# One phase for all ghost FFNs, mLSTM units between the MLP tiles of the block in front, and a look-up spread over six stages

## The chip, the cores and the metric

The kernel runs on one core of a Trainium2 chip. The metric is device time in microseconds of one execution. TensorE is PE in the rows (PEld is its weight load), VectorE is DVE, ScalarE is ACT, GpSimd is POOL, SyncE is SP.

## What is computed

```python
x = L0_attn_x                                # (4, 1024, 512) f32
xn = layernorm(x)
x = x + mlstm_block(xn) + ghost_ffn(xn)

def mlstm_block(x):                          # 8 heads, dqk 32, dv 64
    h_in = rmsnorm(x, norm1_w)
    q, k, v, o_pre = h_in @ wq, h_in @ wk, h_in @ wv, h_in @ w_og
    i_pre, f_pre = softcap(h_in @ w_ig + b_ig), softcap(h_in @ w_fg + b_fg)
    Fcum = cumsum(log_sigmoid(f_pre))
    Dmat = where(causal, Fcum[s] - Fcum[t] + i_pre[t], -inf); m = max_t Dmat
    C = (q @ k.T / sqrt(32)) * exp(Dmat - m)
    h = (C / max(|sum_t C|, exp(-m))) @ v
    x1 = x + (sigmoid(o_pre) * rmsnorm_per_head(h) * mh_w) @ w_out
    h2 = rmsnorm(x1, norm2_w)
    return x1 + (silu(h2 @ w_gate) * (h2 @ w_up)) @ w_down      # 2048 wide

def ghost_ffn(x):                            # 1376 wide; weights are looked up
    g, u = x @ lut[gate_idx].T, x @ lut[up_idx].T               # lut has 16 entries
    return (silu(g) * u) @ lut[down_idx].T
```

## The kernel before, in words

The 4096 rows are taken in eight blocks of 512 rows (`TOK`), two halves for each of four sequences; `at = (b, half)` names one. Everything is fp32 precision on fp32r matmuls: each operand is kept as a rounded part (`hi`) and the remainder (`lo`), and `split` does three matmuls for one product.

Both FFNs are cut into tiles of 128 hidden columns: 11 ghost tiles (`NF`, the last one padded) and 16 MLP tiles (`NM`). A tile is the same for both: `gate` (12 matmuls of 512 columns into `gate_bank`), `up` (12 into `up_bank`), `tanh` on ScalarE, `gated` and `product` on DVE, `hid` on ScalarE (hi part of the hidden) and on POOL (its lo part, line 1757), and `down` (12 into the four accumulators `acc`), which comes one tile later. The weights of a tile, hi and lo, are read from scratch tensors in HBM, 1 MB for gate and up (`load_gu`, line 445) and 0.5 MB for down (`load_dn`, line 450), into two slots each. `load_gu` of tile t+1 waits for `up` of tile t-1.

A stage of a block has three parts. `front`: gate logits, then twelve projections of 128 rows (q and k, v, output gate; line 549 with `attn_w`), and beside them the chain of rows for the exponents (DVE lines 1359 to 1405, ScalarE lines 963 to 1034, transposes on TensorE). The row scratch lies in the x buffer of the other half (`rows`, `og`), so the front waits on DVE until that buffer's output has been stored (lines 1353 to 1356). `ghost`: the 11 ghost tiles of this block; eight mLSTM units (four row blocks, two groups of four heads) run between their matmuls, in an order written out in `units` (line 745): `unit_1` (exponents, scores) after gate, `unit_2` (values) after up, `unit_3` (state) after down, then head transposes, output projection and h2. On DVE the unit's work stands around `gated` and `product` (lines 1558 to 1605). Then come the 16 MLP tiles of the same block on h2, with the layer norm and transposes of the next block's x in the last ones (`mlp_ends`, `x_T`), and at the end DVE adds the accumulators to the residual (`add_out`, line 1641), which ScalarE stores in four transfers (line 1151).

The ghost weights do not exist at the start. They are looked up in 33 chunks of 128x512 (`NCH`: gate, up and down of each tile): ScalarE computes eight levels from bit 0 of the index and pairs of table entries (`level`, line 924), DVE takes the three other bits (line 1281) and chooses with seven `copy_predicated` (line 1302), 10 steps a chunk and one more for bit 0 (line 1293); then ScalarE rounds (`upper`, line 929), POOL subtracts (line 1745) and stores the pair from its own DMA queue (line 1752). `plan` spreads these steps: chunks 0 to 20 in stage 1, 21 to 32 in stage 2, 10 steps in each unit. For that reason stage 1 has no ghost tiles; those of block 0 come last of all (`LAST`, lines 837 to 845 and 1664 to 1671), from its transposed x that is made a second time, and with its rows kept in `first_rows`. The MLP weights are split in stage 1 as well (ScalarE line 937, POOL line 1734, DVE lines 1312 and 1317), the first MLP pass computes from the freshly split tiles, and SP stores them for the later stages. The look-up's work space lies over the projection weights, which are stored once and loaded back (`reload_w`).

SP issues nearly all loads in one queue, in the order of the program: a wait in it holds up every later load. At the end of each second stage SP also waits until the last rows were stored (line 522). All engines run loops over the sequences 1 to 3, so stages 3 to 8 are one code.

## Time and profile before

| | us |
|---|---|
| median of 3 runs | 2777.57 (2776.36 to 2778.02) |
| the profiled execution | 2779.31 |
| its span, first to last instruction | 2777.5 |

| engine | busy us | share of the span |
|---|---|---|
| TensorE, matmuls | 2493.6 | 90% |
| TensorE, weight loads | 2000.8 | 72% |
| DVE | 1295.4 | 47% |
| ScalarE | 809.4 | 29% |
| POOL | 598.7 | 22% |

The shares are means over stages with different limits: a stage has to be read in its own window. In the rows of a timeline the columns are start and length in us, engine, line, operation, output<-input and count; in brackets stands how long the engine was idle before it and which event ended that. Rows with a q behind the engine are what its queue issues, DMAs above all. Line 549 is the helper for all tiled products, so its rows are told apart by the names of the tiles.

### The profile page before, as it was taken

How to read it: one execution, taken by the hardware profiler on the slowest of the kernel's cores; microseconds unless marked ns; L12 is line 12 of the kernel's file. 1: busy time of each engine (PE TensorE's matmuls, PEld its weight loads, DVE VectorE, ACT ScalarE, POOL GpSimd, SP SyncE). 2: the span in 40 equal slices, each digit the busy share in tenths (PEclk: the TensorE clock that was granted, in tenths of full speed). 3: DMA queues.
4: the chain of work that ended last, by engine and by line, in shares of the span. 5: the costliest groups of instructions: out<-in, count | busy, mean ns of one | idle time of the engine just before them, and what ended most of it. 6: DMA issues, size and time to landing. Idle time of an engine off the chain costs nothing.

```text
span 2777.5 us, 32515 instructions
## 1 busy us (share of the span) xinstructions
PE 2493.6 (90%) x11024; PEld 2000.8 (72%) x11024; DVE 1295.4 (47%) x2240; ACT 809.4 (29%) x1474; POOL 598.7 (22%) x497
## 2 busy tenths in 40 slices
PE   4545877677999999999999999999999999999988
PEld 3324656566777788778877788778877888778877
DVE  6886874776134632364125622364235523463221
ACT  4653535552114211321123211321123211321111
POOL 1332540322111211131112211121112211121111
PEclk8757999889999999999999999999999999999999
DMA  5213765335542354244542355135533455135544
GB/s 198 72 46 122 283 235 197 129 122 224 193 173 92 137 189 182 83 141 167 200 153 91 129 197 197 72 134 188 184 128 107 152 189 196 62 138 188 194 182 154
DMA packets 95754, 431.78 MB, mean 155 GB/s; under 512 B 10496, under 2 KB 10496, under 8 KB 65664
## 3 DMA queue, kind: packets, MB, share of 16 engines
q1 hardware_dynamic: 80400, 393.56, 39.3%
q10 hardware_dynamic: 10464, 19.14, 2.1%
q0 software_dynamic: 4752, 17.30, 1.6%
q8 instruction: 78, 1.28, 0.2%
q14 instruction: 60, 0.49, 0.1%
HBM read 371.77 MB, written 58.20 MB: 155 GB/s over the span
## 4 chain that ended last, share of the span: by engine, by line
issue 52%; PE 16%; POOL 9%; ACT 3%; DVE 2%; DMA 2%; POOLq 0%; ACTq 0%; DVEq 0%; SPq 0%
POOL hidden_lo L1757 5%; PE acc L549 4%; PE up_bank L549 3%; PE gate_bank L549 3%; PE bank_b L549 3%; PE bank_a L549 2%; ACT look_w L924 1%; POOL MX L1770 1%; POOL vw L1785 1%; DMA gu<-gu_parts 1%; POOL rh L1702 1%; POOL rs L1702 1%; DMA first_rows<-xn 1%; DVE look_w L1281 0%; PE gate_bank L583 0%
## 5 line engine op out<-in xcount | busy, mean ns | idle before, releaser
L1757 POOL TENSOR_TENSOR hidden_lo<-hm,hidden_hi 128x512 fp32r<-128x512 f32 x216 | 279.6, 1294 | 1504.8 <-ACT hidden_hi L866 1504.7
L549 PE MATMUL acc<-dn,hidden_hi 128*128 128x512 f32 x1728 | 548.0, 399 | 24.6 <-POOL hidden_lo L1757 24.6
L1325 DVE SCALAR_TENSOR_TENSOR th<-th,gate_bank 128x512 f32<-128x512 f32 x216 | 147.8, 684 | 642.6 <-ACT th L861 642.6
L549 PEld LDWEIGHTS acc<-dn,hidden_hi 128*128 128x128 f32 x1728 | 324.0, 191 | 93.1 <-issue 20.2
L866 ACT ACTIVATE hidden_hi<-hm 128x512 fp32r<-128x512 f32 x216 | 135.9, 629 | 848.0 <-PE acc L549 824.2
L549 PE MATMUL gate_bank<-hT_hi,gu 128*128 128x512 f32 x1024 | 340.9, 394 | 30.4 <-DVE hT_lo L1547 19.4
L549 PE MATMUL up_bank<-hT_hi,gu 128*128 128x512 f32 x1024 | 339.7, 393 | 0.7 <-DVE hm L1331 0.6
L549 PE MATMUL acc<-dn,hidden_lo 128*128 128x512 f32 x864 | 339.6, 393 | 0.0
L861 ACT ACTIVATE th<-gate_bank 128x512 f32<-128x512 f32 x216 | 128.8, 596 | 471.8 <-PE gate_bank L549 471.8
L1331 DVE SCALAR_TENSOR_TENSOR hm<-th,up_bank 128x512 f32<-128x512 f32 x216 | 148.0, 685 | 241.6 <-PE up_bank L549 241.0
L549 PE MATMUL up_bank<-xT_hi,gu 128*128 128x512 f32 x704 | 256.8, 426 | 0.0
L549 PE MATMUL gate_bank<-xT_hi,gu 128*128 128x512 f32 x704 | 242.3, 405 | 8.2 <-DMA gu<-gu_parts 8.2
L549 PEld LDWEIGHTS gate_bank<-hT_hi,gu 128*128 128x128 f32 x1024 | 194.0, 189 | 77.1 <-issue 23.5
L549 PEld LDWEIGHTS up_bank<-hT_hi,gu 128*128 128x128 f32 x1024 | 193.1, 189 | 43.3 <-DVE hm L1331 3.3
L924 ACT ACTIVATE look_w<-look_w,lt,ld 128x512 f32<-128x512 int32 x208 | 156.0, 805 | 180.7 <-DMA gu_parts<-look_w 64.7
L549 PE MATMUL gate_bank<-hT_lo,gu 128*128 128x512 f32 x512 | 200.8, 392 | 0.0
L549 PE MATMUL up_bank<-hT_lo,gu 128*128 128x512 f32 x512 | 199.8, 390 | 0.0
L549 PEld LDWEIGHTS acc<-dn,hidden_lo 128*128 128x128 f32 x864 | 164.5, 190 | 35.6
L549 PEld LDWEIGHTS up_bank<-xT_hi,gu 128*128 128x128 f32 x704 | 132.9, 189 | 40.2 <-issue 13.7
L549 PEld LDWEIGHTS gate_bank<-xT_hi,gu 128*128 128x128 f32 x704 | 133.1, 189 | 36.3 <-DMA gu<-gu_parts 8.6
L1302 DVE COPY_PREDICATED look_w<-look_w 128x512 f32<-128x512 int32 x182 | 139.2, 798 | 2.4
L549 PE MATMUL up_bank<-xT_lo,gu 128*128 128x512 f32 x352 | 138.4, 393 | 0.0
(233 smaller groups left out, 3711.3 us busy)
## 6 DMA issues: line engine op xcount, KB each, us to landing
gu<-gu_parts SPq DMA_DIRECT2D x200, 1024.0 KB, 4.8
dn<-dn_parts SPq DMA_DIRECT2D x200, 512.0 KB, 3.4
gu_parts<-gu SPq DMA_DIRECT2D x16, 1024.0 KB, 6.3
gu_parts<-look_w POOLq DMA_DIRECT2D x17, 512.0 KB, 3.1
ix<-idx ACTq DMA_DIRECT2D x33, 256.0 KB, 2.7
raw_gu<-w_gu SPq DMA_DIRECT2D x16, 512.0 KB, 6.9
qkT<-x SPq DMA_DIRECT2D x8, 1024.0 KB, 6.1
xn<-x SPq DMA_DIRECT2D x8, 1024.0 KB, 7.9
```

Source lines behind the costliest of these rows:

```text
L549: mm = pe.matmul(dst, l[a], r[c], start=first and k == 0 and n == 0, stop=last and k == len(lhs) - 1 and n == 2)
L861: act.activation(th[:], GB[:], ACT.Tanh, scale=0.5).then_inc(act_tanh.sem, 1)
L866: act.activation(HH[0][:], hm[:], ACT.Copy).then_inc(act_hid.sem, 1)
L924: act.activation(level_of(n, k), bit0_of(n), ACT.Identity, bias=lt[:, 2 * k:2 * k + 1], scale=ld[:, k:k + 1])\
L1302: dve.copy_predicated(level_of(n, lower), bit_of(n, bit), level_of(n, upper)).then_inc(look_vec, 1)
L1325: dve.scalar_tensor_tensor(th[:], th[:], 1.0, GB[:], ALU.add, ALU.mult).then_inc(vec_gate.sem, 1)
L1331: dve.scalar_tensor_tensor(hm[:], th[:], 0.5, UB[:], ALU.mult, ALU.mult).then_inc(vec_hm.sem, 1)
L1702: pool.tensor_tensor(dst, src, half_pow[:, 0:n], ALU.pow).then_inc(stage.sem, 1)
L1757: pool.tensor_tensor(HH[1][:], hm[:], HH[0][:].bitcast(f32), ALU.subtract).then_inc(pool_hid.sem, 1)
L1770: pool.tensor_tensor(MX[0:n, :, :], mhl[0:n, j * P:(j + 1) * P].unsqueeze(1).to_broadcast([n, H, P]), hm32[0:n, 0:H].unsqueeze(2).to_broad ...
L1785: pool.tensor_tensor(vw[:, u % 2, :, :], va[:, c:c + HG * VS].rearrange("p (h n) -> p h n", h=HG), rn[:, f:f + HG].unsqueeze(2).to_broadca ...
```

## The change

- Two phases. Phase one has a stage per block: `front`, then the 16 MLP tiles of the block **before** it with this block's eight units, output projection and h2 in tiles 0 to 10 (`tiles(at)`, with `mb = previous(at)`). The first stage has units alone, and a `TAIL` of 16 plain MLP tiles ends the phase. Phase two has the 11 ghost tiles of all eight blocks, one after the other; each block's last four tiles carry the transposes of the next block's x.
- x and h2 parts share two pairs of buffers (`XH`), one per half. x1 and the MLP result of a block go to scratch rows in HBM (`x1_rows`, `mlp_rows`); phase two loads x, x1 and MLP rows again, 3 MB a block besides the x of the next, and adds them to the ghost result on DVE in tile 3 and at the end. DVE copies the accumulators out at the end of a stage, and SP stores them in one transfer; the next front waits for it (`st_mlp`).
- The look-up moves from stages 1 and 2 to stages 3 to 8: in each of three pairs of stages one third of the matrices, 5 chunks in even and 6 in odd stages, `TAKEN` DVE steps behind each tile's work: 4 (or 5) in tiles 0 to 7, 4 in tile 8, none in 9 and 10, the rest in 11 to 13. Its space lies over the v and output-gate weights, which are loaded back, 4 MB, at the end of each of these stages. SP stores the chunks in place of POOL, two or more tiles later in its queue.
- The MLP splits stand in stage 1, one in each of tiles 0 to 10, and five in the front of stage 2; all are on ScalarE and POOL now. Stage 2 loads tile 0 back once all are stored.

```diff
-NCH = 3 * NF
-PHASES = [0, 4, 21, 24, NCH]
+NCH = NF
+CHUNKS = [(0, 5), (5, NF)]
+TAKEN = [[4] * 8 + [4, 0, 0, 5, 5, 4, 0, 0], [5] * 8 + [4, 0, 0, 5, 6, 5, 0, 0]]
...
@@ block.sync
+            def tiles(at):
+                b, half = at
+                mb = previous(at)
+                stored = 0
+                for t in range(NM):
+                    if t + 1 < NM:
+                        load_gu(MLP, mb, t + 1)
...
+                    else:
+                        load_gu(MLP, at, 0)
+                    load_dn(MLP, mb, t)
+                    if here(at, TAIL):
+                        continue
+                    if t == 8:
+                        wait(sp, vec_norm, at, NB - 1, "gated")
+                        load_next(at)
+                    if t == 11:
+                        wait(sp, vec_x1, at, NB - 1, "x1")
+                        sp.dma_start(rows_of(x1_rows, (b * HALVES + half) * TOK), XN[half][:]).then_inc(st_x1, 16)
+                    if looks(at):
+                        ready = steps_taken(half, t - 1) // STEPS_V if t else 0
+                        for n in range(CHUNKS[half][0] + stored, ready):
+                            store_chunk(at, n)
+                            stored += 1
+                        if t == NM - 1:
+                            for n in range(*CHUNKS[half]):
+                                if n >= CHUNKS[half][1] - 2:
+                                    pair_stored(sp, at, n)
+                            reload_vo(1)
+                            reload_vo(2)
+                wait(sp, vec_out, mb, NB - 1)
+                first = (b * HALVES + half) * TOK + -TOK
+                sp.dma_start(rows_of(mlp_rows, first), XN[half][:]).then_inc(st_mlp[half], 16)
...
+            sp.wait_ge(st_x1, 16 * BATCH * HALVES)
+            for z in range(2):
+                sp.wait_ge(st_mlp[z], 16 * BATCH)
+                sp.wait_ge(ld_vo[z], 32 + 32 * HALVES * (BATCH - 1))
+            with sp.Fori(BATCH, 2 * BATCH) as b:
+                for half in range(HALVES):
+                    at = (b, half)
+                    for t in range(NF):
+                        if t + 1 < NF:
+                            load_gu(GHO, at, t + 1)
+                        else:
+                            load_gu(GHO, (b, half + 1), 0)
+                        load_dn(GHO, at, t)
+                        if t == 0:
+                            wait(sp, pe_xT, (b, half - 2), NB - 1)
+                            load_next(at)
+                            first = (b * HALVES + half) * TOK + -BATCH * SEQ
+                            sp.wait_ge(st_out[half], b * 16 + (16 - BATCH * 16))
+                            sp.dma_start(rest[half], rows_of(x, first)).then_inc(ld_rest[0], 16)
+                            sp.wait_ge(vec_rest.sem, vec_rest.before(at))
+                            sp.dma_start(rest[2], rows_of(x1_rows, first)).then_inc(ld_rest[1], 16)
+                            sp.dma_start(rest[3], rows_of(mlp_rows, first)).then_inc(ld_rest[2], 16)
+                    wait(sp, vec_out, at, NB - 1)
+                    sp.dma_start(rows_of(out, first), rest[half]).then_inc(st_out[half], 16)
...
@@ block.tensor
+                for t in range(NM):
+                    gate(MLP, mb, t, act, stage)
+                    for f, a in fill.get((t, 0), []):
+                        f(at, a)
+                    up(MLP, mb, t, act, stage)
+                    for f, a in fill.get((t, 1), []):
+                        f(at, a)
+                    if stage and t == NM - 1:
+                        x_T(at, 0, XN[1 - at[1]])
+                        x_T(at, 1, XN[1 - at[1]])
+                    if t:
+                        down(MLP, mb, t - 1, NM - 1)
+                    for f, a in fill.get((t, 2), []):
+                        f(at, a)
...
+            tiles(TAIL)
+            with pe.Fori(BATCH, 2 * BATCH) as b:
+                for half in range(HALVES):
+                    at = (b, half)
+                    act = XH[half]
+                    for t in range(NF):
+                        gate(GHO, at, t, act)
+                        up(GHO, at, t, act)
+                        if t >= NF - NB:
+                            x_T(at, t - NF + NB, XN[1 - half], ghosts=True)
+                        if t:
+                            down(GHO, at, t - 1, NF - 1)
+                    down(GHO, at, NF - 1, NF - 1)
...
@@ block.scalar, at the end of a tile, ahead of the next tile's hid, tanh and exp
+                    if first:
+                        mlp_hi_(t)
+                    if looks(at):
+                        ready = steps_of_levels(at[1], steps_taken(at[1], t - 1) if t else 0)
+                        look_up(at, min(ready, looked + 5) if t < NM - 2 else CHUNKS[at[1]][1] * STEPS_A)
...
@@ block.vector, front, then the end of a tile, behind the unit's state update
+                if here(at, SECOND):
+                    dve.wait_ge(st_x1, 16)
+                elif not first:
+                    dve.wait_ge(st_mlp[1 - half], b * 16)
...
+                    if looks(at):
+                        look_up(at, steps_taken(half, t))
+                    if t == 11:
+                        ln_stats(at, XN[1 - half], 1 - half, b * 16 + (16 + 16 * half))
...
@@ block.gpsimd, a tile, ahead of the next tile's hid
+                    if first:
+                        mlp_lo_(t)
+                    if looks(at):
+                        ready = steps_taken(half, t - 1) // STEPS_V if t else 0
+                        if t == NM - 2:
+                            ready = CHUNKS[half][1]
+                        for n in range(CHUNKS[half][0] + done, ready):
+                            lower(at, n)
+                            done += 1
```

## Rows read from the trace of the kernel before

**Rows 1.** Windows by stage: us; busy of PE, PEld, DVE, ACT, POOL; PEclk, DMA, GB/s.

```profile
23.00:99.50 76.50, 47.21 (x189) 34.36 (x189) 51.63 (x79) 48.38 (x83) 13.38 (x9) 0.84 0.33 123
99.50:222.00 122.50, 53.73 (x134) 31.85 (x135) 109.06 (x178) 74.37 (x126) 40.94 (x33) 0.54 0.19 65
222.00:258.70 36.70, 17.41 (x67) 12.96 (x65) 21.52 (x44) 9.16 (x14) 6.55 (x8) 0.69 0.31 107
431.00:828.40 397.40, 327.06 (x1382) 261.23 (x1381) 207.09 (x357) 144.92 (x250) 85.49 (x74) 0.91 0.45 167
1134.20:1440.00 305.80, 301.29 (x1376) 244.77 (x1374) 123.11 (x224) 72.20 (x142) 58.92 (x49) 1.00 0.40 145
1440.00:1748.00 308.00, 301.72 (x1378) 245.16 (x1379) 123.71 (x226) 72.09 (x142) 58.92 (x49) 1.00 0.43 154
```

**Rows 2.** The same view inside a steady stage: front, unit tiles, plain MLP tiles.

```profile
1440.90:1484.10 43.20, 42.33 (x201) 33.70 (x202) 14.97 (x24) 19.06 (x40) 3.52 (x2) 1.00 0.17 63
1484.10:1613.90 129.80, 126.54 (x586) 101.82 (x585) 75.62 (x142) 31.37 (x66) 32.77 (x29) 1.00 0.44 150
1613.90:1737.30 123.40, 123.40 (x550) 102.14 (x549) 29.43 (x54) 19.49 (x33) 21.37 (x17) 1.00 0.53 191
```

**Rows 3.** The same view of two unit tiles of stage 2, with look-up.

```profile
550.10:570.40 20.30, 13.18 (x51) 10.43 (x51) 15.30 (x26) 9.15 (x18) 6.05 (x5) 0.83 0.36 123
570.40:588.20 17.80, 14.67 (x55) 11.59 (x55) 13.51 (x22) 9.47 (x19) 6.08 (x5) 0.81 0.35 126
```

**Rows 4.** Timeline of two unit tiles of stage 4, and the first MLP gate.

```profile
1198.76 0.69 DVE L1440 TENSOR_TENSOR ar<-bank_a,maskd 128x512 f32<-128x512 f32 x1
...
1201.06 0.70 PE L621 MATMUL bank_b<-kv,qkT 128*128 128x260 f32 x2 [0.57 <-DVE ct L1447]
...
1209.31 0.69 DVE L1440 TENSOR_TENSOR ar<-bank_a,maskd 128x512 f32<-128x512 f32 x1 [1.67 <-PE bank_a L607]
...
1212.73 0.60 PE L621 MATMUL bank_b<-kv,qkT 128*128 128x260 f32 x2
...
1302.99 0.49 PE L549 MATMUL gate_bank<-hT_hi,gu 128*128 128x512 f32 x1 [0.93 <-DVE hT_lo L1547]
```

**Rows 5.** DVE's look-up steps: busy us, mean ns, idle; then min/median/max ns by line.

```profile
L1302 DVE COPY_PREDICATED look_w<-look_w 128x512 f32<-128x512 int32 x182 | 139.2, 798 | 2.4
...
L1302 DVE COPY_PREDICATED look_w<-look_w x182: 701/743/3257, 105.2 to 655.2; 128x512 f32<-128x512 int32 x182
L1281 DVE TENSOR_SCALAR look_w<-ix x78: 404/422/4365, 101.2 to 649.5; 128x512 int32<-128x512 int32 x78
```

**Rows 6.** MLP split and its load; the first layer norm of the run.

```profile
L1734 POOL TENSOR_TENSOR gu<-raw_gu,gu x16: 2327/2402/2891, 191.6 to 411.7; 128x1024 fp32r<-128x1024 f32 x16
...
raw_dn<-w_dn SPq DMA_DIRECT2D x15, 256.0 KB, 3.9
...
6.99 2.47 DVE L1198 BATCH_NORM_STATS2 st<-xn 128x6 f32<-128x512 f32 x4 [6.99 <-DMA xn<-x]
```

**Rows 7.** Timeline of the last seam, from MLP tiles to ghost tiles, and the end.

```profile
2668.09 2.48 DVE L1641 TENSOR_TENSOR xn<-xn,acc 128x512 f32<-128x512 f32 x4 [2.64 <-PE acc L549]
...
2673.38 0.38 SPq L531 DMA_DIRECT2D qkT<-first_rows  x1
...
2673.80 0.76 SPq L445 DMA_DIRECT2D gu<-gu_parts  x1
...
2681.67 0.79 PE L549 MATMUL gate_bank<-xT_hi,gu 128*128 128x512 f32 x1 [8.18 <-DMA gu<-gu_parts]
...
2767.58 1.19 PE L549 MATMUL acc<-dn,hidden_hi 128*128 128x512 f32 x2 [2.21 <-POOL hidden_lo L1757]
```

**Rows 8.** DMA issues (count, KB, us to landing), and a window with full queues.

```profile
gu<-gu_parts SPq DMA_DIRECT2D x200, 1024.0 KB, 4.8
...
gu_parts<-gu SPq DMA_DIRECT2D x16, 1024.0 KB, 6.3
...
675.00:686.00 11.00, 10.12 (x52) 8.23 (x51) 7.14 (x12) 3.62 (x7) 1.41 (x2) 1.00 1.00 423
```

More of the change, by code:

```diff
@@ new lines, in up, with down @@
+            def up(of, at, t, act, stage=None):
+                z = slot(of, at, t)
+                if t == 0 and stage:
+                    wait(pe, vec_rows, stage, 0, "factors")
+                else:
+                    wait(pe, of.hm, at, t - 1)
+                split(UB[:], [(WGU[:, z, 1, 0, toks(k)], WGU[:, z, 1, 1, toks(k)]) for k in range(KT)],
+                      [pair(act, S_, k, S_) for k in range(KT)]).then_inc(of.up.sem, 1)
+            def down(of, at, t, last):
+                z = slot(of, at, t)
+                if t == 0:
+                    pe.wait_ge(vec_out.sem, vec_out.before(at))
+                pe.wait_ge(ld_dn[z], loads(of, at, t))
+                wait(pe, of.low, at, t, "lo")
@@ L838, in _ @@
-            for t in range(NF):
-                gate(LAST, t, t % 2, XT, loads(LAST, t))
-                up(LAST, t, t % 2, XT)
-                if t:
-                    if t == 1:
-                        pe.wait_ge(vec_out.sem, vec_out.before(LAST))
-                    down(LAST, t - 1, (t - 1) % 2, loads(LAST, t - 1), first=t == 1)
-            down(LAST, NF - 1, (NF - 1) % 2, loads(LAST, NF - 1), last=True)
+                    front((b, half))
+                    tiles((b, half))
+            tiles(TAIL)
@@ new lines, in tiles @@
+                if stage:
+                    for i in range(NB):
+                        x_T(at, i)
+                if first:
+                    return
+                wait(dve, MLP.down, mb, NM - 1)
+                if stage:
+                    dve.wait_ge(st_x1, b * (16 * HALVES) + (16 * half + 16))
+                else:
+                    wait(dve, pe_xT, previous(at), NB - 1)
+                for i in range(NB):
+                    dve.tensor_copy(XN[half][:, i, :], ACC[i][:]).then_inc(vec_out.sem, 1)
```

1166 lines of the change are left out of this document (481 added, 685 removed).

## The prediction

> **What bounds the kernel now.** I read windows cut at the stages first. Six of the eight stages are alike, 305.8 or 308.0 us, with TensorE busy over 98% of them at full clock; the first two take 431.0 and 397.4 us at a granted clock of 0.54 to 0.91 [rows 1]. Then the same view inside a steady stage: the front (projections, gate rows) 43.2 us from its first matmul to the first ghost tile's tanh, eleven ghost tiles with the mLSTM units 129.8 us, and fifteen steps of plain MLP tiles 123.4 us, of which two transposes are 1.0: 8.16 a tile [rows 2]. So TensorE bounds the steady part, and only the first 828 us are loose: there the look-up on DVE and the weight splits compete with the units.
>
> **What the change does to the total work.** All 128 MLP tiles, 88 ghost tiles, 64 units and 8 fronts stay. The gain can only come from stages 1 and 2, the price from where tiles and units meet the look-up, and from each new seam between blocks.
>
> **1. Stage 1 without look-up.** It starts its gate matmuls at 23.0 as now [rows 1]. Front: 43.2 in the steady state [rows 2], 2 more at the half clock of the start, 3 for the output weights: units begin at 71, against 99.5. The stretch of the units takes 122.5 us now, 15.3 each [rows 1]; one chunk per unit costs DVE 7 selections of 0.74 and 4 bit steps of 0.42, 6.9 us [rows 5], so 8.4 each is the floor if all of it was serial and 15.3 the ceiling; walking the unit's chain at half clock (mask, exp, weights, values, heads, and the norm of every second unit) gives me 11.8: 94 us, to 165. The end of the stage takes 36.7 now [rows 1]; ScalarE stood about 10 us of it behind look-up work, so 27: to 192. Now the next block's layer norm and transposes come in the open: the same chain runs from 7.0 to 23.0 at the start [rows 6], 16 us: to 208. The MLP splits (POOL 2.4 us for a gate/up pair [rows 6]) sit under the unit chain of 11.8. Bounds for the 208: 180 with 8.4 a unit, 236 with 15.3.
>
> **2. Stage 2.** Its front carries the last five splits on ScalarE's queue. A down tile can be loaded only after the previous one is split (load 3.9 us, POOL 1.3 and 2.4 [rows 6]), 7 us a round, and ScalarE's instructions behind it wait: 9 us more. Then the last split has to be stored (6.3) and loaded back (4.8) [rows 8] before the first gate matmul, 11 us more. First tanh at 208 + 43.2 + 2 + 9 + 11 = 273 (if all hidden 253, if each round is exposed 290). Units with tiles, no look-up: 129.8, and four plain steps 32.6: 435.6.
>
> **3. Six steady stages.** Eleven tiles of 8.16 leave each: 306.9 (mean of the two rows) - 89.8 = 217.1; the wait for h2 ahead of the MLP tiles (0.93 [rows 4]) goes, the seam costs 0.3 more: 216.5, six times 1299. The front's row chain now waits for one 1 MB store of the MLP rows, issued from SP after the accumulators are copied and behind 4 MB of reloaded v/o weights. The reload is issued about 9 us before the block's last matmul and at 423 GB/s [rows 8] takes 10, so the store lands some 9 us after that matmul, where the chain needs it at 8, with 1.9 of slack ahead of the next transposes: nothing, up to 2 per stage if the reload is late. What hides it is 43 us of projections.
>
> **4. The look-up in them.** Four steps after each unit tile in even stages, five in odd: 2.8 and 3.5 us of DVE by [rows 5], 2.9 and 3.6 with the waits between steps. They stand behind the unit's state update and ahead of the next unit's mask on DVE, in a queue that looks idle for 4 us a tile but idles elsewhere. Going into an even tile DVE starts the mask with no idle time (1198.76), and TensorE already waits 0.57 us for the weights that follow (1201.06) [rows 4]: the whole 2.9 or 3.6 lands on TensorE. Going into an odd tile DVE idles 1.67 and TensorE's value matmul (1212.73) starts without a wait, with 1.2 to spare [rows 4]: 0 and 0.6. Three such pairs, and 2.0 or 2.7 before the last head transpose: 11 and 15.5 us. In the odd stages two lo-subtractions on POOL wait for a ScalarE step that comes one tile later; POOL's next hidden_lo waits behind, 2 us each, 4. The pauses reach 3.5 and 4.2 us: the clock of the tiles with look-up in stage 2 was 0.83 and 0.81 [rows 3], and a fall costs about 1.7: 4.5 and 5. Together 15.5 and 24.5, 40 a block, **120** for three. As a check, those tiles with ten steps each took 20.3 and 17.8 us against 23.6 for a steady pair (two elevenths of 129.8), 0.73 per step; mine is 40 us for the 72 steps that a block has in its eight unit tiles, 0.56. Ends: 10 if it all fits DVE's idle time, 180 at 0.73 for each of three times 72 steps (158) and POOL's waits on top.
> The Trainium skill (SBUF — State Buffer, the rules on the shared port) says that a DVE instruction with two SBUF inputs and a GpSimd one that reads SBUF lock each other out for a whole instruction. The selection steps are such; their mean of 798 ns over a median near 743 may be that. Estimated with one hit per tile it would be 30 us more; by the trace's mean it is in the sum.
>
> **5. The MLP tail.** From the last tanh of stage 8 to its last down matmul 11.7; sixteen plain tiles 130.6, and 2.2 where the last down waits for hidden_lo [rows 7]. The seam: SP stands at the end of a stage until the accumulators have been copied, and only then loads the gate/up weights of tile 1; before, a front hid that, now TensorE is there after gate and up of tile 0, 5.4 us. This is what the last seam shows today: SP issues a 1 MB load and then tile 1's weights, and TensorE stands 8.18 us [rows 7]. Load after copies 2.6, issue and a 1 MB store ahead 7.8 (2673.80 to 2681.67): 10.8, so 5.3 of standing and 1.9 for the half clock after it. Tail: 140, ending at 435.6 + 1299 + 120 + 11.7 + 140 = 2006.
>
> **6. Eight ghost blocks.** Matmuls 11 x 8.16, transposes of the next block 2.0: 91.8, eight times 734. Each seam: 2.2 for the last hidden_lo and 1.0 of clock (the four downs after it run slow in [rows 7]); 5.4 for tile 1's weights as above, 1.9 of clock; then SP has put x for the next block, x, the x1 rows and the MLP rows, 4 MB, ahead of tile 2's weights. 7.5 MB at about 0.4 MB/us plus 2 of latency end at 25, where TensorE wants tile 2 at 21: 4.1, and 1.2 of clock. 15.8 a seam. The first is worse by 4: SP also waits until the MLP rows' store has landed (6 to 8 us) before it loads. 8 x 15.8 + 4 = 131, and 3 for the loop's turns. What hides the residual adds and the layer norm is DVE's idle time, 6 of 8 us a tile. Ends: 30 if tile 1's and 2's loads are in time, 180 if the rows load slower.
> **7. The end.** Adds 2.5, then a 1 MB store instead of four small ones: 9.4.
>
> **Sum:** 2006 + 734 + 131 + 3 + 9.4 = **2884 us**. It is a span; the profiled run of before is 2777.5 in span and 2779.3 in time, the median of the runs 2777.57, so I set them equal. Against now: stages 1 and 2 save about 150 us; look-up 120, the seams of the ghost blocks 131 and the tail's 7 give it back and more.
>
> **Rivals.**
> **A, faster: the look-up rides free.** DVE is busy 75.6 of 129.8 us in the unit tiles [rows 2], so 35 to 40 us of steps fit by sum. If the queue shifts as a whole into its idle places, the 120 are gone: 2764. It decides at 3.3 us a stage: above that there is no gain. Against it: the 0.57 of TensorE behind DVE in [rows 4], and the stage-2 tiles, which took 7 us more per chunk with DVE idle a quarter of the time [rows 3]. 8%.
> **B, about even: the seams are hidden.** If the loads pass the stores and the row loads, 12.6 a seam and 7 of the tail go: 2884 - 112 = 2772. The 8.18 us in [rows 7] and the load of 4.8 alone [rows 8] speak against it. 9%. Both A and B: 2652, 3%.
> **C, slower: the clock.** If every unit tile with look-up runs as in [rows 3], TensorE busy 13.2 and 14.7 where a tile needs 11.5, the 48 tiles give 2.4 each, 115, of which 28 are in the sum: 2971. The full clock of all steady stages [rows 1] speaks against it, as these have no pauses. 15%. The Trainium skill's advice (TensorE: Matmul & The Clock Gate, "Why this matters for your kernels") is to leave no idle gaps between bursts of matmuls, and this change adds them; the slow downs after a 2.21 us wait in [rows 7] agree.
> **D: the change doesn't do what it says**, units and MLP tiles serialize on some wait: tile 0's gate waits for h2 of its block, long done; I find none. 2%, far above 2971.
>
> **Chances.** The forecast 63%, its own range 2830 to 2940. A 8, B 9 (a third on each side and a third even), A and B 3, C 15, D 2. A run of this kernel tells 0.2% (5.6 us) from no change. Faster 14%, same 4%, slower 82%. The range 2765 to 2955 leaves out A's lower part, both together, C's upper part and D.
>
> **What would show it.** Right: stages 3 to 8 between 230 and 243 us, alternating, with TensorE waiting for ct and DVE for nothing there; a stage-2 first tanh near 273; in the ghost phase 107 to 108 us a block with one wait of 5 to 6 us for gate weights at tile 1 and a shorter one at tile 2, and half clock after each. Wrong: TensorE over 97% busy in unit tiles (A), no DMA wait at the seams (B), a clock under 0.9 over whole stages (C), or a first stage near 260, which would mean that its chain was never DVE's.

## The result

The changed kernel takes **2890.79 us** (median of four runs, 2881.09 to 2907.21) against 2777.41 for the kernel before beside it (2776.36 to 2778.02): 1.0415 times as long, 95% interval 1.0367 to 1.0463. The forecast was 2884, slower. Its own runs scatter by 26 us, those of before by 2; the profiled execution, 2881.09 us with a span of 2879.3, is the fastest of the four.

Windows cut where the first tanh of a stage starts (the first one at the first gate matmul of stage 2's front) show where the time is. Columns: stretch and us; busy us of PE, PEld, DVE, ACT, POOL; granted clock, DMA share, GB/s. In order: stage 2's front; stage 2 with stage 3's front; stages 3 and 4 with the fronts behind them; the MLP tail; one ghost block of eight.

```profile
195.80:262.90 67.10, 49.61 (x201) 37.85 (x202) 15.36 (x21) 26.49 (x50) 21.89 (x12) 0.83 0.53 196
...
262.90:477.50 214.60, 211.49 (x981) 171.03 (x981) 107.76 (x200) 58.84 (x120) 44.66 (x38) 1.00 0.40 134
477.50:710.70 233.20, 218.41 (x982) 175.35 (x982) 145.20 (x253) 89.57 (x166) 55.71 (x43) 0.97 0.45 157
710.70:952.80 242.10, 216.77 (x982) 172.69 (x981) 149.51 (x265) 94.91 (x175) 56.34 (x44) 0.99 0.43 155
...
1867.80:2011.00 143.20, 134.84 (x577) 110.72 (x576) 24.48 (x36) 19.63 (x32) 20.58 (x16) 0.96 0.53 185
...
2120.10:2229.40 109.30, 98.59 (x413) 80.01 (x412) 32.57 (x56) 15.91 (x26) 16.26 (x13) 0.94 0.58 207
```

The steady stages, 305.8 and 308.0 us with eleven ghost tiles more in [rows 1], should take 217 without them; they take 233 and 242. Stage 2, where the units have no look-up beside them, does take 215 with the front behind it, at full clock. A ghost block takes 109.3 where its matmuls and transposes need 91.8. The groups of the whole run name the three waits of TensorE (columns: busy us, mean ns; then idle us ahead, by what ended it):

```profile
L561 PE MATMUL gate_bank<-act_hi,gu 128*128 128x512 f32 x1728 | 605.4, 412 | 99.5 <-DMA gu<-ghost_parts 71.7 <-DMA gu<-mlp_parts 25.5 <-issue 2.2
...
L561 PE MATMUL acc<-dn,hidden_hi 128*128 128x512 f32 x1728 | 559.7, 406 | 32.5 <-POOL hidden_lo L1648 32.5
...
L634 PE MATMUL bank_b<-kv,qkT 128*128 128x260 f32 x128 | 51.9, 492 | 88.5 <-DVE ct L1358 88.2
```

Stage 3's waits ahead of its even tiles answer [rows 4] and [rows 5]. Timeline of after: start, us, engine, operation, and in brackets the idle time before it.

```profile
501.88 0.76 DVE L1244 COPY_PREDICATED look_w<-look_w 128x512 f32<-128x512 int32 x1
...
502.79 1.96 DVE L1244 COPY_PREDICATED look_w<-look_w 128x512 f32<-128x512 int32 x3 [0.15 <-DVE look_w L1244]
...
504.64 0.68 DVE L1351 TENSOR_TENSOR ar<-bank_a,maskd 128x512 f32<-128x512 f32 x1
...
506.92 1.23 PE L634 MATMUL bank_b<-kv,qkT 128*128 128x260 f32 x2 [3.32 <-DVE ct L1358]
...
536.21 0.60 PE L634 MATMUL bank_b<-kv,qkT 128*128 128x260 f32 x1 [3.40 <-DVE ct L1358]
...
563.52 0.61 PE L634 MATMUL bank_b<-kv,qkT 128*128 128x260 f32 x1 [2.43 <-DVE ct L1358]
```

Four selections, 2.76 us, stand ahead of the mask, and TensorE's 0.57 us wait of [rows 4] is 3.32: 2.75 more, where the prediction had 2.9. The other two are 2.8 and 1.9 more. The next two matmuls take 1.23 us instead of 0.70, and the window behind the wait shows the lower clock:

```profile
506.90:511.50 4.60, 4.58 (x15) 4.01 (x16) 2.63 (x5) 0.25 (x1) 0.00 (x0) 0.50 0.17 71
```

A seam of the ghost blocks answers [rows 7]:

```profile
2119.98 0.41 SPq L544 DMA_DIRECT2D result<-look_w  x1
2120.50 0.44 SPq L432 DMA_DIRECT2D gu<-ghost_parts  x1
...
2125.85 2.54 SPq L542 DMA_DIRECT2D look_w<-mlp_rows  x1
2128.51 2.36 SPq L432 DMA_DIRECT2D gu<-ghost_parts  x1
...
2127.98 0.79 PE L561 MATMUL gate_bank<-act_hi,gu 128*128 128x512 f32 x1 [5.19 <-DMA gu<-ghost_parts]
...
2142.59 0.49 PE L561 MATMUL gate_bank<-act_hi,gu 128*128 128x512 f32 x1 [3.41 <-DMA gu<-ghost_parts]
```

The waits of 5.19 and 3.41 were forecast as 5.4 and 4.1, in that order and behind those loads. Over the eight blocks they are 3.3 to 6.7 and 3.3 to 4.9.

### The profile page after: what moved, and what is told of

It reads as the page before. It is cut to its first block, busy times and chain, and to the rows that moved or that the text cites. A ratio compares the mean times of both kernels' runs of the same rounds, so it can differ in the third digit from the quotient of the medians.

```text
span 2879.3 us, 33321 instructions
## 1 busy us (share of the span) xinstructions
PE 2558.6 (89%) x11152; PEld 2045.8 (71%) x11152; DVE 1382.3 (48%) x2444; ACT 837.6 (29%) x1522; POOL 628.6 (22%) x496
## 4 chain that ended last, share of the span: by engine, by line
PE 44%; issue 38%; POOL 7%; DVE 6%; DMA 2%; ACT 2%; DVEq 0%; POOLq 0%; SPq 0%; ACTq 0%
PE acc L561 10%; PE up_bank L561 9%; PE gate_bank L561 8%; PE bank_b L561 5%; PE bank_a L561 5%; POOL hidden_lo L1648 4%; PE bank_a L637 2%; PE bank_b L634 1%; PE bank_a L596 1%; DMA gu<-mlp_parts 1%; DVE look_w L1244 1%; PE bank_b L644 1%; PE bank_b L626 1%; DMA raw_dn<-w_dn 1%; POOL vw L1679 1%
## 5 line engine op out<-in xcount | busy, mean ns | idle before, releaser
L561 PE MATMUL gate_bank<-act_hi,gu 128*128 128x512 f32 x1728 | 605.4, 412 | 99.5 <-DMA gu<-ghost_parts 71.7
L561 PE MATMUL up_bank<-act_hi,gu 128*128 128x512 f32 x1728 | 593.9, 405 | 0.0
L561 PE MATMUL acc<-dn,hidden_hi 128*128 128x512 f32 x1728 | 559.7, 406 | 32.5 <-POOL hidden_lo L1648 32.5
L561 PEld LDWEIGHTS gate_bank<-act_hi,gu 128*128 128x128 f32 x1728 | 341.1, 197 | 184.5 <-issue 105.5
L561 PEld LDWEIGHTS up_bank<-act_hi,gu 128*128 128x128 f32 x1728 | 326.7, 189 | 80.9 <-issue 13.5
L561 PE MATMUL gate_bank<-act_lo,gu 128*128 128x512 f32 x864 | 350.8, 406 | 0.0
L561 PE MATMUL up_bank<-act_lo,gu 128*128 128x512 f32 x864 | 338.6, 392 | 0.0
L561 PEld LDWEIGHTS up_bank<-act_lo,gu 128*128 128x128 f32 x864 | 163.4, 189 | 46.5 <-issue 13.4
L561 PEld LDWEIGHTS gate_bank<-act_lo,gu 128*128 128x128 f32 x864 | 171.2, 198 | 34.9
L634 PE MATMUL bank_b<-kv,qkT 128*128 128x260 f32 x128 | 51.9, 492 | 88.5 <-DVE ct L1358 88.2
L1664 POOL TENSOR_TENSOR MX<-mhl,hm 40x1024 fp32r<-40x1024 f32 x32 | 66.0, 2063 | 197.5 <-DVE mhl L1308 191.9
```

The source lines that it names most:

```text
L561: mm = pe.matmul(dst, l[a], r[c], start=first and k == 0 and n == 0, stop=last and k == len(lhs) - 1 and n == 2)
L634: pe.matmul(B[:, 0:HG * VS], qkT[:, 0, g, toks(j)], kv[:, g, :, :], start=True, stop=True)
L1664: pool.tensor_tensor(MX[0:n, :, :], mhl[0:n, j * P:(j + 1) * P].unsqueeze(1).to_broadcast([n, H, P]), hm32[0:n, 0:H].unsqueeze(2).to_broad ...
```

## The experiments

Medians of four or five runs are given. The kernel before, run beside each set, took 2780 to 2783 us. The kernel after was not run again beside them: its 2890.8 stands beside a before of 2777.4, and scatters by 26, so a difference to it of 10 us or less says little by itself.

**Is it the look-up, and whose part of it?** no_look leaves out every step of it; VectorE's share of the edit:

```diff
...
-                    if looks(at):
-                        look_up(at, steps_taken(half, t))
...
```

> The kernel after without any look-up in the six stages: the steps on VectorE, the levels and the upper half on ScalarE, the lower half on GpSimd, the index loads and the chunk stores are left out, and the ghost tiles read MLP weights in place of looked-up ones, so the ghost part of the output is another, with the same number and size of loads. Theory (the look-up's place in the queues pauses TensorE): in the trace of after, the sixteen tiles of stages 3 to 8 take 179, 186, 178, 188, 178 and 191 us from tanh to tanh, and those of stage 2, which have the units and no look-up, 160.6; the difference, 137 us, should go: 2754 us, all six stages at 160 to 163. Rival 1 (units between tiles pause TensorE by themselves, and the look-up is only there at the same time): stages near 172, 2825 us. Rival 2 (most of the rise is not in these stages at all): above 2850.

Measured: 2747.0 (2743.8 to 2754.8), ratio to before 0.988 [0.9863, 0.9897]. From first to last tanh the sixteen tiles take 161.1 to 161.5 in all six stages. The look-up costs 144 us, and its rivals 1 and 2 fall. Without it the change would be a gain of 1.2%. Its stages 3 and 4, to be held beside those of after:

```profile
474.90:689.90 215.00, 211.14 (x981) 170.71 (x980) 107.00 (x198) 58.87 (x120) 44.73 (x38) 1.00 0.44 152
689.90:906.90 217.00, 211.34 (x981) 170.63 (x981) 107.32 (x199) 58.87 (x120) 44.73 (x38) 1.00 0.43 151
```

Of the 18.2 us that stage 3 loses (233.2 less 215.0), 7.3 are PE busy longer, 218.41 less 211.14, at the same count of matmuls: the clock. The other 10.9 are pauses. In stage 4 it is 5.4 of 25.1.

vec_only keeps VectorE's steps and drops ScalarE's, GpSimd's and the transfers:

```diff
-                dve.wait_ge(ld_idx[n % 2], count(at, 16 * (NCH - NCH // 2 if n % 2 == 0 else NCH // 2), 16 * (n // 2 + 1)))
...
-                    dve.wait_ge(look_act, count(at, 8 * NCH, 8 * n + (2, 4, 0, 8, 8)[step - 3]))
...
-                        look_up(at, min(ready, looked + 5) if t < NM - 2 else CHUNKS[at[1]][1] * STEPS_A)
```

> As no_look, but VectorE's steps stay: bit steps and selections in the same number, the same size and at the same places, on other data (so what the look-up gives is left out, and the ghost tiles read MLP weights). ScalarE's levels, GpSimd's lower half, index loads and chunk stores are gone. Theory (steps stand in VectorE's queue ahead of the next mask): even stages keep 15 to 18 us of their 18, odd ones 20 to 24 of their 28, as only GpSimd's and ScalarE's order goes: 2754 + 105 to 125, so 2860 to 2880. Rival 1 (ScalarE and GpSimd carry it: levels ahead of tanh, lower half ahead of hidden_lo): under 2790. Rival 2 (DMA traffic of chunks and indices): under 2770.

Measured: 2897.9 (2896.4 to 2899.3). VectorE's steps alone bring the whole loss, 151 us; both rivals fall. But my own range was missed too: nothing came back for ScalarE's and GpSimd's share in the odd stages. Its TensorE waits 124.1 us for ct, after's 88.2, no_look's 33.0.

**GpSimd's wait.** act_six asks about that share in the real kernel:

```diff
-                        look_up(at, min(ready, looked + 5) if t < NM - 2 else CHUNKS[at[1]][1] * STEPS_A)
+                        look_up(at, min(ready, looked + 6) if t < NM - 2 else CHUNKS[at[1]][1] * STEPS_A)
```

The wait meant, in an odd stage of after: the chunk's lower half stands ahead of hidden_lo on GpSimd until ScalarE comes to the upper half, and TensorE pauses 2.57 us.

```profile
755.81 0.63 ACT L928 ACTIVATE look_w<-look_w 128x512 fp32r<-128x512 f32 x1
...
756.51 1.27 POOL L1643 TENSOR_TENSOR look_w<-look_w 128x512 fp32r<-128x512 f32 x1 [17.55 <-ACT look_w L928]
757.74 1.26 POOL L1648 TENSOR_TENSOR hidden_lo<-hm,hidden_hi 128x512 fp32r<-128x512 f32 x1
...
759.15 0.70 PE L561 MATMUL acc<-dn,hidden_hi 128*128 128x512 f32 x2 [2.57 <-POOL hidden_lo L1648]
...
761.62 1.52 ACT L923 ACTIVATE look_w<-look_w,lt,ld 128x512 f32<-128x512 int32 x2 [4.48 <-DMA ghost_parts<-look_w]
```

> The kernel after with one number changed: ScalarE may do six levels a tile, not five, so that the upper halves of the first two chunks of an odd stage come in the tile in which GpSimd waits for them, not one later. The prediction put this wait at 4 us an odd stage, 12 in all: 2879. In the trace of look_mid each such wait holds VectorE 4.3 us and TensorE 2.6, and one tile later ScalarE waits 4.4 us for a chunk's store and TensorE 2.7 for weights whose load stands behind that store on SyncE's queue: if the second wait hangs on the first, 8 to 10 us an odd stage, 24 to 30 in all: 2861 to 2867. Rival (the pause is taken by the steps on VectorE anyway): 2885 to 2895.

Measured: 2883.7 (2876.9 to 2887.6), 7 less than after and within after's scatter. The same groups of its trace say why:

```profile
L561 PE MATMUL gate_bank<-act_hi,gu 128*128 128x512 f32 x1728 | 601.7, 410 | 89.9 <-DMA gu<-ghost_parts 73.3 <-DMA gu<-mlp_parts 14.3 <-issue 2.3
L561 PE MATMUL acc<-dn,hidden_hi 128*128 128x512 f32 x1728 | 564.5, 409 | 19.2 <-POOL hidden_lo L1648 19.2
L634 PE MATMUL bank_b<-kv,qkT 128*128 128x260 f32 x128 | 52.7, 499 | 105.7 <-DVE ct L1358 105.5
```

The wait for hidden_lo fell from 32.5 to 19.2, no_look's value, and that for MLP weights from 25.5 to 14.3; the wait for ct rose from 88.2 to 105.5. While TensorE stood for GpSimd, VectorE's steps passed for nothing. Of the 24.5 us of waits that went, 17 came back, and the odd stages take 563.2 from tanh to tanh in sum where after's take 564.8. So the term of 12 us was no full addition: it and the steps share one pause. The expected 24 to 30 us were missed; whether 7 us or nothing is gained, these runs don't decide.

**Where in VectorE's queue?** look_free and look_late put the steps of each pair of unit tiles in one place:

```diff
-TAKEN = [[4] * 8 + [4, 0, 0, 5, 5, 4, 0, 0], [5] * 8 + [4, 0, 0, 5, 6, 5, 0, 0]]
+TAKEN = [[6, 0, 6, 0, 6, 0, 6, 0, 5, 0, 0, 7, 8, 6, 0, 0], [7, 0, 7, 0, 7, 0, 7, 0, 6, 0, 0, 8, 9, 9, 0, 0]]
```

> The same look-up with its steps at other places: after even unit tiles 6 (even stages) or 7 (odd stages), after odd unit tiles none, after tile 8 five or six, after tiles 11 to 13 seven, eight, six and eight, nine, nine. ScalarE may do up to 9 levels a tile, not 5. Theory (VectorE's queue has 2.9 us to spare ahead of the mask of an odd unit tile and none ahead of that of an even one): 4.3 or 5.0 us of steps leave 1.5 to 2.1 four times, tile 8 two, the plain tiles one each, some clock: 12 and 16 us a stage instead of 18 and 28, together 85 instead of 137: 2840. Rival (each step costs the same wherever it stands, by contention or clock): 2880 to 2900, and look_late the same.

> As look_free with one thing changed: the six or seven steps of each pair of unit tiles stand after the odd one, ahead of the mask of an even one. Theory: 4.3 or 5.0 us stand fully on TensorE's path, three times ahead of a mask and once in front of the last head transpose, with a fall of the clock behind each (1.7): 29 and 33 us a stage, 186 together: 2940, 100 us above look_free. Rival (the same cost wherever a step stands): within 15 us of look_free.

Measured: 2912.7 (2907.9 to 2915.0) and 2954.9 (2948.7 to 2965.8). The order is as expected, the size not: 42 us apart instead of 100, and look_free 22 above after instead of 50 below. In look_late the selections are prolonged less (a mean of 847 ns, look_free's 1002), and still it is the slower: the place in the queue counts by itself. But the "free" place wasn't free. In its even stages tile 0's six steps cost 1.2 us, as worked out (1.5), but those of tiles 2 and 4 6.7 and 7.2. There, VectorE and GpSimd side by side:

```profile
509.53 2.91 DVE L1244 COPY_PREDICATED look_w<-look_w 128x512 f32<-128x512 int32 x2
512.60 3.06 DVE L1244 COPY_PREDICATED look_w<-look_w 128x512 f32<-128x512 int32 x2 [0.15 <-DVE look_w L1244]
```

```profile
509.49 1.29 POOL L1648 TENSOR_TENSOR hidden_lo<-hm,hidden_hi 128x512 fp32r<-128x512 f32 x1 [6.48 <-ACT hidden_hi L860]
510.74 1.09 POOL L1679 TENSOR_TENSOR vw<-va,rn 128x260 f32<-128x260 f32 x1
511.80 2.37 POOL L1664 TENSOR_TENSOR MX<-mhl,hm 40x1024 fp32r<-40x1024 f32 x1
```

A selection takes 1.5 us instead of 0.75 there, and GpSimd's own instructions are stretched, vw from 0.62 to 1.09. free_port makes GpSimd's two large ones narrow:

```diff
+                n = 8 if of is MLP and looks(at) else TOK
+                pool.tensor_tensor(HH[1][:, 0:n], hm[:, 0:n], HH[0][:, 0:n].bitcast(f32), ALU.subtract).then_inc(of.low.sem, 1)
...
+                    w = 4 if looks(at) else P
```

> look_free with GpSimd's two large instructions made narrow in the stages with look-up: the low half of the hidden tile on 8 of 512 columns and the mask rows of four columns of each block, so these parts of the output are left out; their counts, order and waits stay. In look_free a selection took 745 ns with GpSimd idle or in its square roots, and about 1580 beside the low half of the hidden tile or the mask rows; 231 of them took 1002 on average, 60 us over 745. Theory A (the two engines hold each other up at the memory): selections back at 745, 2913 falls to 2850 to 2865. Rival (a step's own time and place set the pause, the doubled ones stand in idle time): within 10 us of look_free.

Measured: 2810.6 (2804.9 to 2813.3), 102 less than look_free; the mean of a selection fell from 1002 to 790 ns. In look_free, then in free_port:

```profile
L1244 DVE COPY_PREDICATED look_w<-look_w 128x512 f32<-128x512 int32 x231 | 222.9, 1002 | 16.5 <-DVE look_w L1244 9.5 <-DVE look_w L1222 0.5
```

```profile
L1244 DVE COPY_PREDICATED look_w<-look_w 128x512 f32<-128x512 int32 x231 | 174.3, 790 | 17.7 <-DVE look_w L1244 9.5 <-ACT look_w L923 1.2 <-DVE look_w L1222 0.5
```

The rival falls; the fall is larger than the selections' 49 us, and than theory A's 48 to 63. TensorE's wait for ct falls from 105.5 to 52.3, so the time is gained where VectorE's queue is waited for; no matmul of look_free waits for the mask rows, and the wait for hidden_lo changes by 1.3 us alone. With the collisions gone, the place is as free as worked out: the six steps behind tiles 2 and 4 cost 1.6 and 1.8 us in an even stage. Part of the 102 is not the look-up's: tiles 2, 4 and 6, with no step ahead, take 11.6 us where look_free's and no_look's take 12.4, some 14 us in the six stages. after_port makes the same edit to after itself:

> The kernel after with GpSimd's low half of the hidden tile and its mask rows made narrow in the stages with look-up (8 of 512 columns, 4 of each block's 128), as in free_port; that part of the output is left out, counts, order and waits stay. In the trace of after the 231 selections hold 22 us over 745 ns each, of 99 in look_free's 60; that edit took 102 us from look_free, 1.7 for each us of selections. Theory (the prediction had put these collisions into its mean and at nothing beyond it): 22 to 38 us, 2853 to 2869. Rival (collisions in after stand in idle time of VectorE): 2885 to 2895.

Measured: 2822.3 (2821.1 to 2831.5), 69 less than after, far beyond my 22 to 38. I had counted the selections alone. Summed over the six stages VectorE is busy 64 us less: selections 15.3, the state update kv 16.9, bit steps 13.0, one instruction of the gate rows 8.0, the rest small ones. The state update stands ahead of the mask as the selections do. Two of them in after, beside hidden_lo and alone:

```profile
731.14 1.28 POOL L1648 TENSOR_TENSOR hidden_lo<-hm,hidden_hi 128x512 fp32r<-128x512 f32 x1 [8.83 <-ACT hidden_hi L860]
731.37 1.35 DVE L1382 SCALAR_TENSOR_TENSOR kv<-kv,rn,tt 128x260 f32<-128x260 f32 x1
...
543.20 0.49 DVE L1382 SCALAR_TENSOR_TENSOR kv<-kv,rn,tt 128x260 f32<-128x260 f32 x1
```

Some of the 69 was there without the look-up (no_look's kv has a mean of 821 ns, after's 845), and a narrow hidden_lo also comes sooner: the wait for it falls by 6.4 us, that for ct by 35.2. The runs don't divide it further. What they show is that the prolonged instructions don't stand in idle time.

**Another place in the queue.** look_mid moves three steps of each unit tile behind the addition of the heads:

```diff
                         unit_2(t)
+                        if looks(at):
+                            look_up(at, (steps_taken(half, t - 1) if t else CHUNKS[half][0] * STEPS_V) + 3)
```

> The kernel after with the same number of look-up steps in each tile, but three of the four or five of each unit tile stand between VectorE's addition of the heads and its state update, where it idles 2.3 us a tile in the trace of no_look (waiting for the state matmul behind the down matmuls) and GpSimd is idle too; only one or two stay ahead of the next mask. Theory (what costs is a step that stands ahead of a mask): the three fit in the 2.3 us, the rest costs 0.75 a step in front of even tiles: 3 and 6 us, with the clock 5 and 10, and the order of GpSimd's work in odd stages 4: about 55 for the six stages instead of 137: 2810. Rival 1 (each step costs about 1.1 us wherever it stands, 137 us over some 120 steps in the unit tiles): 2880 to 2900. Rival 2 (the order of ScalarE and GpSimd alone sets it): above 2870.

Measured: 2819.6 (2813.7 to 2827.8), 71 less than after with as many steps in the same tiles; both rivals fall. An even stage takes 219.4, 4.4 more than in no_look, an odd one 236.9, 19.9 more, where I had 14. Fewer collisions with GpSimd, another reason for a gain at this place, are not it: the selections have a mean of 863 ns here and 837 in after.

```profile
477.00:696.40 219.40, 211.64 (x981) 170.60 (x980) 144.00 (x253) 89.49 (x166) 54.77 (x43) 1.00 0.48 167
696.40:933.30 236.90, 218.15 (x982) 172.96 (x981) 149.95 (x265) 95.10 (x175) 55.00 (x44) 0.98 0.43 158
```

Here GpSimd's wait stands in the open, no longer hidden by the steps, and one tile on the next load is late behind the chunk's store on SyncE's queue (start 746.37, 2.65 us):

```profile
740.28 0.70 PE L561 MATMUL acc<-dn,hidden_hi 128*128 128x512 f32 x2 [2.57 <-POOL hidden_lo L1650]
...
742.65 1.52 ACT L923 ACTIVATE look_w<-look_w,lt,ld 128x512 f32<-128x512 int32 x2 [4.38 <-DMA ghost_parts<-look_w]
...
746.37 0.79 PE L561 MATMUL gate_bank<-act_hi,gu 128*128 128x512 f32 x1 [2.65 <-DMA gu<-mlp_parts]
```

**The seams.** seam_gu issues tile 1's weights before the wait for the accumulators; seam_rows moves the four row loads behind the weights of tiles 2 to 4; seam_both does both.

```diff
+                        if t + 1 == NF:
+                            load_gu(GHO, (b, half + 1), 1)
...
-                        if t == 0:
+                        if t == 1:
                             wait(sp, pe_xT, (b, half - 2), NB - 1)
                             load_next(at)
+                        if t == 2:
                             first = (b * HALVES + half) * TOK + -BATCH * SEQ
```

> The kernel after with the ghost phase's load queue in another order: SyncE issues the gate/up weights of the next block's tile 1 before it waits for the accumulators to be copied, and the four 1 MB loads of rows one at a time behind the weights of tiles 2, 3 and 4 (the residual adds then follow tile 5, not 3). Theory (order of the queue): the waits of 5 to 6 us at tile 1 and 3 to 5 at tile 2 with their clock go at seven seams, 12.5 each, and 5 at the first one: 2891 - 92 = 2799. Rival 1 (the memory's rate is the limit, the bytes only move): 2870 or more, with waits at tiles 3 to 5 instead. Rival 2 (at a seam the last down's wait for hidden_lo and the clock after it are most of the 16 us): 2855.

> As seam_both with the first part alone (tile 1's weights ahead of the wait; the 4 MB of rows stay where they are). Theory: the wait at tile 1 goes, but tile 2's weights still stand behind the rows and come only about 2.5 us earlier, while TensorE is there 7 us earlier: 3 a seam, 2870. Rival (bandwidth, the rows can't be the cause): the same as seam_both within 5 us.

> The kernel after with the second part of seam_both alone: the four 1 MB loads of rows go one at a time behind the weights of tiles 2, 3 and 4, the residual adds after tile 5; tile 1's weights still wait for the accumulators to be copied and stand behind the store. Theory (each wait has its own place in the queue): the first step of a ghost block keeps its 13.4 us, the second falls from 12.1 to 15 to 8.2, eight times 5.3: 42 us, 2849; seam_gu's 10 and these 42 leave another 42 of seam_both's 94 that only the two together save, as in seam_gu the wait moved to tile 2 (19.5 us there). Rival (the rows are the whole seam): within 10 us of seam_both, 2797.

Measured: 2797.2 (2788.4 to 2798.6), 2881.1 (2874.6 to 2882.7) and 2850.7 (2841.6 to 2850.9). From after's 2890.8: both 94, the first alone 10, the second alone 40, and 44 that only the two together give. As after's runs scatter, the traces are the better measure: from the first ghost tanh to the end 868.3 us in after, 860.6 in seam_gu, 823.6 in seam_rows, 778.6 in seam_both, so seam_gu gains 8, seam_rows 45, seam_both 90, and 37 come of the two together. seam_both and seam_rows came as expected (2799, 2849); seam_gu did not (2870), but all rivals fall. seam_gu's one remaining wait, then a block of seam_both and one of seam_gu as windows (in seam_gu that wait is 9.2 to 9.4 in seven blocks; the first block keeps both waits):

```profile
2141.29 0.79 PE L565 MATMUL gate_bank<-act_hi,gu 128*128 128x512 f32 x1 [9.39 <-DMA gu<-ghost_parts]
```

```profile
2122.60:2218.50 95.90, 93.70 (x413) 76.65 (x412) 32.59 (x56) 15.90 (x26) 16.41 (x13) 0.98 0.65 236
```

```profile
2121.10:2227.90 106.80, 94.31 (x413) 76.78 (x412) 32.60 (x56) 15.92 (x27) 16.33 (x13) 0.95 0.61 214
```

The 5.19 us at tile 1 went, and the 3.41 at tile 2 became 9.39: TensorE came sooner to weights that come when the queue lets them. The same bytes in another order do without either wait, at 236 GB/s against after's 207, so it was never the rate.

**All together.** best joins seam_both and look_mid and adds a new spread of the steps (none of the extra ones behind odd tiles in even stages, GpSimd nowhere ahead of ScalarE) and an earlier load for stage 2:

```diff
+TAKEN = [[4, 3, 4, 3, 4, 3, 4, 3, 4, 0, 0, 6, 6, 6, 0, 0], [4, 4, 4, 4, 4, 4, 4, 4, 6, 0, 0, 8, 8, 6, 0, 0]]
...
+                if m == NM - 1:
+                    sp.wait_ge(st_gu[0], 16 * (NM // 2))
+                    load_gu(MLP, FIRST, 0)
```

> All that helped, together: ghost load queue as in seam_both, also for the first ghost block; three steps of each unit tile in VectorE's idle place as in look_mid; steps spread anew so that only one step stands after a unit tile (none after odd ones in even stages), more after plain tiles, and GpSimd nowhere waits one tile for ScalarE; the weights of stage 2's first tile loaded as soon as the last store on its own slot has landed (in the trace of after TensorE waits 7.3 us there). Sum: no_look's 2747, less 94 for the seams as measured in seam_both, less 6 for the first ghost block, less 7 for stage 2's first tile, and 5 an even stage and 10 an odd one for what is left of the look-up, 45: 2685. Rival 1 (the savings overlap, as load and look-up share the queues): 2730. Rival 2 (the plain tiles cannot hold six or eight steps each): 2720.

Measured: **2676.6** (2672.8 to 2681.3), 0.9628 [0.9615, 0.9641] of before: it beats both kernels, and its rivals (2730, 2720) fall. No run takes its new parts one by one. From first to last tanh an even stage takes 162.8 and an odd one 168.1, no_look's 161.1 and 161.5 plus 1.7 and 6.6. The fronts behind the odd stages are longer too: from stage 2's last tanh to stage 8's it is 1326.4 us, no_look's 1295.5 and after's 1429.8, so 31 us of look-up are left of 134. Stages 3 and 4:

```profile
472.10:688.80 216.70, 211.41 (x982) 170.68 (x981) 140.97 (x253) 89.68 (x166) 54.33 (x43) 1.00 0.47 169
688.80:916.00 227.20, 213.73 (x982) 170.71 (x981) 150.40 (x265) 95.58 (x175) 56.08 (x44) 0.99 0.47 165
```

DVE is nearly as busy in them as in after (there 145.20 and 149.51); TensorE's busy time is within 0.3 and 2.4 us of no_look's.

## Why the prediction was right, and which of its terms were off

By its own steps, against the trace of after:

| step | predicted | measured |
|---|---|---|
| 1, second block's front begins | 208 | 195.9 |
| 2, first tanh of stage 2 | 273 | 262.9 |
| 2, its tiles to the last tanh | 162.6 | 160.6 |
| 3 and 4, to stage 8's last tanh | 1419 | 1429.8 |
| 5, to the tail's last down | 151.7 | 155.0 |
| 6, eight ghost blocks | 868 | 863.6 |
| 7, the end | 9.4 | 7.4 |
| span | 2884 | 2879.3 |

The sum lies closer to the span than its terms, and that is luck: stage 1 was put 12 us too long, steps 3 and 4 together 11 too short, and the rest together 3 too long.

**Step 1** was mis-sized. The units begin at 66 for 71, take 90 for 94, and the end of the stage with the next block's transposes takes 40 for 43. **Step 2's** front was nearly right as a whole, 67.0 for 65, with 17.4 us of waits for the 20 given to splits, last store and load: 7.05 and 3.12 behind ScalarE's splits for 9, and 7.26 for the weights for 11. PE is busy 7.3 longer than in [rows 2] at a clock of 0.83, where 2 were given:

```profile
195.86 0.61 PE L561 MATMUL up_bank<-act_hi,gates_w_hi 128*16 128x512 f32 x1 [1.41 <-DVE act_lo L1189]
...
223.12 0.66 PE L596 MATMUL gate_bank<-ident,vw 128*128 128x128 f32 x2 [7.05 <-ACT qkT L967]
...
242.80 0.74 PE L561 MATMUL bank_b<-vo_w_hi,act_hi 128*128 128x512 f32 x1 [3.12 <-ACT th L984]
...
257.42 0.76 PE L561 MATMUL gate_bank<-act_hi,gu 128*128 128x512 f32 x1 [7.26 <-DMA gu<-mlp_parts]
```

best's earlier load takes the last wait to 5.12, not to nothing. Its first tanh comes at 257.7; but 4.4 us of that are an earlier start of the front (191.5), which vec_only has as well (191.4) with this code unchanged.

**Step 3** held: no_look's six stages take 1295.5 from stage 2's last tanh to stage 8's, 215.9 each, for 216.5. **Step 4** was right in kind and 12% low in size: with tanh-to-tanh 17.6 to 18.7 in even stages and 24.9, 27.4 and 30.7 in odd ones over stage 2's 160.6, in sum 137 for 120. That the steps' place in the queue makes these pauses is shown by look_mid, and the alternation was as forecast. The parts against no_look:

| us | predicted | measured |
|---|---|---|
| stage 3, pauses | 11 | 10.9 |
| stage 3, clock | 4.5 | 7.3 |
| stage 4, VectorE's steps | 15.5 | 9.4 |
| stage 4, GpSimd's wait | 4 | 4.4 |
| stage 4, MLP weights behind a store | 0 | 4.6 |
| stage 4, clock | 5 | 5.4 |

Another 1.2 us of stage 4's pauses lie in the front behind it. So in even stages the price of the clock was too low: no row shows the 1.7 us that a fall was priced at, and stage 3 pays 7.3 for three waits of 2.4 to 3.4. Its pauses are spread otherwise, too: into even tiles 7.4 for 8.7, into odd ones 2.5 for nothing, ahead of the last head transpose 0.9 for 2. In stage 4 the sum was right with wrong terms: the steps cost less, as they share pauses with GpSimd's wait (act_six), and the wait for MLP weights, put at nothing, took their place. Stages 6 and 8 lose more, 27.1 and 29.8. The collisions with GpSimd, put at nothing beyond the mean of [rows 5], make the steps and VectorE's other work longer: the 231 selections of after hold 22 us over 745 ns each, and the edit that removes these and the others gives 69. The 137 lie between the ends given, 10 and 180.

The Trainium skill (SBUF — State Buffer, "Who interferes with whom") states that a VectorE instruction with two SBUF inputs and a GpSimd one that reads SBUF hold each other up for a whole instruction. The prediction priced it at 30 us and took it as contained in the mean of a selection. The traces agree with the rule: kv 0.49 and 1.35 us, selections 0.75 and 1.5. It also states that the one that issues first has its way and the other blocks; that fits GpSimd's vw, which left selections at 0.73 us where it came second and was itself stretched from 0.62 to 1.1. The rule deserved a term of its own.

**Steps 5 and 6** stand nearly as worked out (the tail took 3 us more, the ghost blocks 4 less): tile 1's 5.19 for 5.4, tile 2's 3.41 for 4.1, 107.3 to 109.3 a block for 107.6. That the two waits are one queue, so that mending the first alone moves most of it to the second, is shown by the three seam kernels and follows from the arrival time of 25 us that step 6 worked with. Small slips in the sums: in step 5, 2.6 and 7.9 are 10.5, not 10.8; in step 6, 8 x 15.8 + 4 is 130, not 131; rival A's gain over the kernel before ends at 2.3 us a stage (2777.6 less 2764, over six stages), not at 3.3.

**The rivals.** A, a free ride of the look-up, would have had 2764, and B, hidden seams, 2772; neither came by itself, and look_mid and seam_both had to be written to get near them. C would have had 2971; the clock of whole stages was 0.96 to 0.99, and its share of the loss, 7.3 of 18.2 us in stage 3, was in the price of each pause. For D there was no sign.

What stays open: how much of after_port's 69 us a kernel without look-up would gain as well, and why after's own runs differ by up to 26 us. The traces show where, not why: the three seam kernels have after's code in stages 3 to 8, and their even stages all take 178.1 to 179.5 from tanh to tanh, but stage 4 takes 194 where after's profiled execution has 185.5.

## What to carry to other kernels

Idle time of an engine is worth nothing at the place where its queue is full: find for each step the instruction that it delays, and put it behind the one that waits for somebody else anyway; with the same work in the same tiles, that was 71 of 144 us here. Two waits on one queue, or on one path, don't add: remove one and look at the next before believing the sum. When a loop is cut in two, issue the next turn's first loads ahead of the wait that closes this one, and what is needed late behind them.

## What the runs showed of the hardware

How VectorE and GpSimd hold each other up could be read instruction by instruction. In the trace of after, instructions of VectorE that overlap none of GpSimd's have medians of 751 ns (selections), 490 (state update) and 419 (bit steps, one SBUF input). Where GpSimd's hidden_lo or mask rows started first, VectorE's instruction ended a fixed time behind GpSimd's end: 0.28 to 0.29 us for the state update (26 of 26, median 1347 ns in all) and for bit steps (six beside the mask rows, 2118 ns in all), 0.61 to 0.63 for selections (17 of 18, median 1584 ns). So the cost is what is left of GpSimd's instruction, and not a factor of two. Where VectorE's started first, it kept its time, and GpSimd's was stretched: hidden_lo from 1.29 to 1.50 us beside selections, the mask rows from 1.89 to 2.15 beside bit steps. GpSimd's square roots cost VectorE nothing (selections 0.74 us). Instructions of VectorE that take one input from a PSUM bank did not change beside hidden_lo: the gating of th 687 ns, the mask 679. I had not expected the bit steps in this list. The same section of the Trainium skill names tensor_scalar in its two-port mode among those that take the shared pair; the 2118 ns agree with it, but no run here shows in which mode the bit steps ran.
